# Another order of the steps of all five engines, and other PSUM banks, in a mixer and feed-forward kernel on one core

## The reference, cut to what matters

```python
# x: 4 batches of 512 rows of 512; W1, W3: 2048 x 512; W2: 512 x 2048
def mixer(h, Wi, Wf, Wg, Wo, gnorm_w):
    i, f, g = h @ Wi.T, h @ Wf.T, h @ Wg.T
    gate = sigmoid(f)
    v = silu(i) * (1 - gate)
    o = scan over the rows t of a batch: o[t] = gate[t] * o[t-1] + v[t]
    o = o * rsqrt(mean(o * o) + eps) * gnorm_w * g * sigmoid(g)
    return o @ Wo
def ffn(x, W1, W2, W3):
    hidden = silu(x @ W1.T) * (x @ W3.T)
    hidden = fwht(hidden)                  # Walsh-Hadamard over 2048, / sqrt(2048)
    return hidden @ W2.T
x = x + layernorm(mixer(layernorm(x)))
return x + layernorm(ffn(layernorm(x)))
```

## Time and profile before

| what | value |
|---|---|
| time, median of 3 runs | 689.96 us (690.3, 688.73, 689.96) |
| profiled execution, its time | 689.71 us |
| profiled execution, its span | 687.9 us |
| TensorE busy | 656.9 us (95%) |
| VectorE busy | 409.8 us (60%) |
| ScalarE busy | 352.8 us (51%) |
| GpSimd busy | 234.1 us (34%) |
| mean granted clock of TensorE | 0.995 |
| moved by DMA | 114.12 MB |

### The profile page before, as it was taken

How to read it: one execution, slowest core, us unless ns; L and a number is a source line. 1 busy time by engine, 2 the same in 40 slices (tenths; PEclk the granted TensorE clock), 3 DMA queues, 4 the chain that set the end, 5 groups by cost and what they waited for, 6 DMA issues and landing times.

```text
span 687.9 us, 11542 instructions
## 1 busy us (share of the span) xinstructions
PE 656.9 (95%) x4339; PEld 427.8 (62%) x4340; DVE 409.8 (60%) x791; ACT 352.8 (51%) x629; POOL 234.1 (34%) x216
## 2 busy tenths in 40 slices
...
GB/s 318 406 404 103 129 117 62 61 7 179 122 160 132 169 280 146 329 300 113 266 274 174 111 108 108 136 299 224 108 108 126 170 134 192 146 120 200 3 1 91
DMA packets 60743, 114.12 MB, mean 166 GB/s; under 512 B 40464, under 2 KB 40720, under 8 KB 56080
## 3 DMA queue, kind: packets, MB, share of 16 engines
...
...
## 4 chain that ended last, share of the span: by engine, by line
PE 64%; DVE 16%; ACT 7%; issue 5%; DVEq 3%; DMA 2%; POOL 2%; SPq 0%; POOLq 0%; ACTq 0%
PE ps L635 21%; PE ps L636 21%; PE ps L637 21%; DVEq L1052 3%; DVE st L1051 2%; ACT junk L914 1%; DVE o_s L1142 1%; ACT ring L835 1%; DMA out<-res 1%; DVE w2t L1306 1%; DVE w2t L1311 1%; DVE mv L1053 1%; ACT junk L921 1%; POOL w2t L1406 1%; DVE ring L1251 1%
## 5 line engine op out<-in xcount | busy, mean ns | idle before, releaser
L635 PE MATMUL ps<-xb,ring 128*128 128x256 f16 (+1 forms) x704 | 212.6, 302 | 3.5 <-DVE ring L1094 1.6
L637 PE MATMUL ps<-xb,ring 128*128 128x256 f16 (+1 forms) x704 | 212.6, 302 | 0.0
L636 PE MATMUL ps<-xb,ring 128*128 128x256 f16 (+1 forms) x704 | 212.6, 302 | 0.0
L1421 POOL TENSOR_TENSOR ring<-sga,ring 128x512 f16<-128x512 f32 x64 | 78.5, 1232 | 316.9 <-ACT ring L1007 316.9
L635 PE MATMUL ps<-ring 128*128 128x256 f16 x384 | 105.2, 274 | 4.4 <-DVE ring L1281 4.3
L636 PE MATMUL ps<-ring 128*128 128x256 f16 x384 | 105.0, 274 | 0.0
L637 PE MATMUL ps<-ring 128*128 128x256 f16 x384 | 105.0, 273 | 0.0
L635 PE MATMUL ps<-w2t,ring 128*128 128x512 f16 x256 | 97.0, 379 | 3.2 <-POOL ring L1421 3.2
L637 PE MATMUL ps<-w2t,ring 128*128 128x512 f16 x256 | 97.0, 379 | 0.0
L636 PE MATMUL ps<-w2t,ring 128*128 128x512 f16 x256 | 97.0, 379 | 0.0
L635 PEld LDWEIGHTS ps<-xb,ring 128*128 128x128 f16 x704 | 69.1, 98 | 40.8 <-issue 3.7
...
## 6 DMA issues: line engine op xcount, KB each, us to landing
...
```

Of the source, the lines that this page charges most:

```text
L635: pe.matmul(dst, a_hi, b_hi, start=start, stop=False, skip_group_check=onto)
L636: pe.matmul(dst, a_hi, b_lo, start=False, stop=False, skip_group_check=onto)
L637: return pe.matmul(dst, a_lo, b_hi, start=False, stop=stop, skip_group_check=onto)
L1421: pool.tensor_tensor(hid(b, c, 1), sga[:, c % 2], hid(b, c, 0), ALU.subtract).then_inc(hid_lo, 1)
```

## The change

Only the five tables differ (L38 to L179). They hold the same steps. Their order differs on every engine, and many products have another bank. A line or two of the tables, from the first feed-forward batch change and from the end:

```diff
 PE_ORDER = """
...
-GQ.1.4:4 D.1.7 GP.1.5:6 GU.1.3 GR.1.4 GU.1.4 GQ.1.5:5 D.1.8 D.1.9 D.1.10 D.1.11 D.1.12 D.1.13 GR.1.5 GP.1.6:7 D.1.14
+GQ.1.2:4 D.0.62 GR.1.2 GU.1.1 GP.1.3:7 D.0.63 GU.1.2 GQ.1.3:5 GP.1.4:6 GR.1.3 GQ.1.4:4 D.1.0 D.1.1 GP.1.5:7 GR.1.4
+D.1.2 D.1.3 GU.1.3 D.1.4 D.1.5 D.1.6 GU.1.4 GQ.1.5:5 D.1.7 GP.1.6:6 GR.1.5 D.1.8 D.1.9 GQ.1.6:4 GU.1.5 GR.1.6 D.1.10
...
+D.3.37 D.3.38 GQ.3.15:5 D.3.39 GR.3.15 D.3.40 D.3.41 D.3.42 GU.3.15 D.3.43 D.3.44 D.3.45 D.3.46 D.3.47 D.3.48 D.3.52
 DVE_ORDER = """
...
-W.0.1 GU.1.2 GR.1.3 GU.1.3 W.0.2 W.0.3 UP.1.2 Z1.3.0 Z1.3.1 Z2.3.0 Z2.3.1 Z1.3.2 UP.1.3 GR.1.4 Z1.3.3 GU.1.4 Z2.3.2
+W.0.1 V.0.3 W.0.2 GR.1.3 GU.1.3 UP.1.2 W.0.3 GR.1.4 GU.1.4 Z1.3.0 UP.1.3 Z2.3.0 Z1.3.1 Z1.3.2 Z2.3.1 Z2.3.2 ZT.3.0
```

More of the change, by code:

```diff
@@ L44 @@
[L44 to L48, removed]
@@ new lines @@
+F.0.2:5 I.0.0:6 I.0.1:0 I.0.2:1 F.0.3:7 XT.1.2:2 G.0.0:3 G.0.1:6 G.0.2:5 I.0.3:4 G.0.3:2 XT.1.3:3 H2.0.0:0 H2.0.1:7
+F.1.0:6 G.1.0:1 I.1.0:5 MS.0.0:3 Y.0.0:4 Y.0.1:2 Y.0.2:3 Y.0.3:6 F.1.1:4 WS.0.0:1 I.1.1:5 G.1.1:2 F.1.2:1 I.1.2:4
+G.1.2:3 F.1.3:6 I.1.3:5 F.2.0:2 W2S.0.0:1 G.1.3:4 I.2.0:3 G.2.0:6 F.2.1:5 H2.1.0:2 H2.1.1:1 H2.2.0:0 H2.2.1:4 MS.1.0:7
+Y.1.0:3 Y.1.1:6 Y.1.2:5 Y.1.3:2 I.2.1:1 G.2.1:0 F.2.2:4 I.2.2:7 H2.3.0:3 H2.3.1:6 G.2.2:5 F.2.3:2 I.2.3:1 F.3.0:0
+G.2.3:4 I.3.0:7 G.3.0:5 MS.2.0:3 Y.2.0:2 Y.2.1:6 H2.4.0:0 Y.2.2:1 H2.4.1:4 Y.2.3:7 F.3.1:5 I.3.1:3 G.3.1:2 F.3.2:0
@@ new lines @@
+H2.5.0:4 H2.5.1:6 I.3.2:5 G.3.2:1 F.3.3:7 I.3.3:0 GP.0.0:6 G.3.3:3 GP.0.1:7 H2.6.0:2 GQ.0.0:4 GQ.0.1:5 GR.0.0 GR.0.1
+H2.6.1:1 MS.3.0:0 Y.3.0:3 Y.3.1:2 GP.0.2:6 GU.0.0 GU.0.1 GP.0.3:7 H2.7.0:1 Y.3.2:0 GQ.0.2:4 H2.7.1:3 Y.3.3:2 GR.0.2
+GQ.0.3:5 GP.0.4:6 GR.0.3 GU.0.2 D.0.0 GU.0.3 GP.0.5:7 D.0.1 GQ.0.4:4 D.0.2 D.0.3 D.0.4 D.0.5 GR.0.4 D.0.6 GQ.0.5:5
+D.0.7 GR.0.5 GU.0.4 D.0.8 D.0.9 D.0.10 D.0.11 GP.0.6:6 GU.0.5 D.0.12 GP.0.7:7 D.0.13 GQ.0.6:4 D.0.14 D.0.15 GR.0.6
+GQ.0.7:5 D.0.16 GR.0.7 D.0.17 D.0.18 D.0.19 GU.0.6 GU.0.7 GP.0.8:6 GP.0.9:7 GQ.0.8:4 D.0.20 D.0.21 D.0.22 GR.0.8
@@ new lines @@
+D.1.33 GR.1.12 D.1.34 D.1.35 GU.1.12 GP.1.13:7 D.1.36 D.1.37 GQ.1.13:5 D.1.38 GR.1.13 D.1.39 D.1.40 GU.1.13 GP.1.14:6
+GP.1.15:7 GQ.1.14:4 GQ.1.15:5 GR.1.14 D.1.41 GR.1.15 D.1.42 D.1.43 D.1.44 GU.1.14 D.1.45 D.1.46 D.1.47 GU.1.15
+GP.2.0:6 D.1.48 D.1.49 D.1.50 GP.2.1:7 D.1.51 D.1.52 GQ.2.0:4 D.1.53 D.1.54 D.1.55 D.1.56 GR.2.0 GU.2.0 GP.2.2:6
+D.1.57 D.1.58 GQ.2.1:5 D.1.59 GR.2.1 GU.2.1 D.1.60 GP.2.3:7 D.1.61 D.1.62 D.1.63 GQ.2.2:4 GQ.2.3:5 GR.2.2 GR.2.3
+GU.2.2 GP.2.4:6 GU.2.3 GP.2.5:7 GQ.2.4:4 D.2.0 D.2.1 GQ.2.5:5 GR.2.4 D.2.2 GR.2.5 D.2.3 GU.2.4 GP.2.6:6 GU.2.5 D.2.4
@@ new lines @@
+GP.2.7:7 D.2.5 D.2.6 GQ.2.6:4 D.2.7 GQ.2.7:5 D.2.8 GR.2.6 D.2.9 GU.2.6 D.2.10 GR.2.7 D.2.11 D.2.12 GU.2.7 GP.2.8:6
+D.2.13 GP.2.9:7 D.2.14 GQ.2.8:4 D.2.15 D.2.16 D.2.17 GR.2.8 GQ.2.9:5 D.2.18 GR.2.9 GP.2.10:6 D.2.19 GU.2.8 D.2.20
+D.2.21 GU.2.9 GQ.2.10:4 D.2.22 D.2.23 GP.2.11:7 D.2.24 GR.2.10 D.2.25 GU.2.10 GP.2.12:6 D.2.26 GQ.2.11:5 D.2.27
+GR.2.11 D.2.28 GU.2.11 D.2.29 GP.2.13:7 D.2.30 GQ.2.12:4 D.2.31 GR.2.12 D.2.32 D.2.33 D.2.34 GP.2.14:6 D.2.35 GU.2.12
+GQ.2.13:5 D.2.36 D.2.37 D.2.38 GQ.2.14:4 D.2.39 GR.2.13 D.2.40 D.2.41 GU.2.13 GP.2.15:7 D.2.42 GR.2.14 D.2.43
@@ L88 @@
[L88 to L90 removed]
+XT.0.0 XT.0.1 AQ.0.0 XT.0.2 XT.0.3 AQ.1.0 AQ.2.0 AT.0.0 AT.0.1 AQ.3.0 AT.0.2 AT.0.3 F.0.0 AT.1.0 AT.1.1 F.0.1 AT.1.2
+XT.1.0 AT.1.3 AT.2.0 AT.2.1 WN.0.0 AT.2.2 WN.1.0 AT.2.3 I.0.0 AT.3.0 I.0.1 AT.3.1 XT.1.1 WN.2.0 F.0.2 S.0.0 I.0.2
```

199 lines of the change are left out of this document (90 added, 109 removed).

## The result

The changed kernel takes 685.15 us (median of 7 runs, 683.37 to 687.67) against 689.96 (7 runs, 688.73 to 691.63). The ratio is 0.9932, with a 95% interval of 0.9912 to 0.9952: some 4.7 us faster. That lies inside the range, 677.8 to 686.0, and 4.2 us above the forecast of 681.0. The profiled execution took 684.75, with a span of 683.0.

A forecast was written before the change was run, and what follows sets the result against it. TensorE, busy 656.9 of 687.9 us, bounds the kernel, so an order can win only the other 31.0. 687.9 - 5.8 - 3.4 - 0.5 + 1.0 = 679.2 us of span, with 1.8 around it 681.0 us; range 677.8 to 686.

The forecast's parts named there:

- The end: TensorE's wait on GpSimd before D.3.56, after GU.3.15: seven D steps kept for this place cover it, -3.4 us.
- The middle: TensorE's wait before GU.1.4: copies moved ahead of the statistics on VectorE win 4.4 plus 1.4 of lower clock, -5.8 us.
- rival B: Batch change: late reloads hold VectorE at W.0.3 or Z1.3.3, giving back 2 to 5.8 us; 683 to 687, chance 0.14.
- The forecast's own interval: Whole kernel: the forecast holds at 679.5 to 682.5 us, chance 0.60.
- the signs named: TensorE: no wait over 1 us after 82, clock 1.00 from 20 us, D.3.56 right behind D.3.52, waits near 15 us.
- The clock: TensorE's lower clock after the middle wait loses 1.4 us, booked as won; the end's 3.2 us wait cost no clock.
- The front: Up to 82 us: VectorE's chain sets TensorE, so 0 booked, with bounds of -0.8 and +0.8 us.
- Small waits: ScalarE's copies holding TensorE between 195 and 275 us: -0.5 us booked.
- the 1.0: Products closer together: 0.2 us each at GP.1.2, GP.2.2, GP.3.2, plus 0.4 at the last batch change, +1.0 us.
- rival E: VectorE, tight in 200 to 290 us: its stretching grows and is exposed, making the kernel slower, near 691.5; chance 0.04.

The follow-up runs named there:

- b_end: Kernel before with seven D steps kept back until after GU.3.15 on TensorE; 688.89 us against 691.23, ratio 0.9967.
- a_end_undone: Changed kernel with the seven D steps put back in front of GU.3.15 on TensorE; 688.66 us, ratio 0.9958 to the kernel before.
- b_copies_first: Kernel before with the copies GR.1.4 and GU.1.4 moved ahead of the statistics (Z1.3.0) on VectorE; 694.71 us against 691.23, ratio 1.0055.
- b_slot_late: Kernel before with the load of weight slot WL.1.3 moved from ahead of O.0.0 to behind LZ.3.2 on SyncE; 692.12 us, ratio 0.9996.
- a_up_first: Changed kernel with UP.1.3 moved ahead of Z1.3.0 on VectorE; 686.44 us, ratio 0.9938 to the kernel before.
- a_copies_back: Changed kernel with the copies GR.1.4 and GU.1.4 put back behind Z1.3.2 on VectorE; 689.51 us, ratio 0.9962 to the kernel before.

## Why the prediction was right in its range and wrong in one step

**The end: right.** -3.4 was booked, and the column "end" fell from 3.40 to 0.10. b_end and a_end_undone show it from both sides. What the prediction took for safe, that such a wait doesn't cost the clock, was wrong (below), so where the lower clock follows the wait, the step is worth 1.5 to 1.8 us more (4.90 with 3.40 of wait in b_copies_first, 5.08 with 3.39 in b_slot_late, 4.84 with 3.06 in a_end_undone).

**The middle: the step that failed.** The prediction said of the statistics that "what waits for them is the input of the third batch", and booked -5.8. It followed GR.1.4, GU.1.4 and then GR.1.5, but not UP.1.3, which the new table puts behind Z1.3.0 on VectorE. Through UP.1.3 the seed of GP.1.5, and so GQ.1.5, waits for the first reload; the excerpt of the changed order shows it (L1332 behind the first L1051). UP.1.3 once moved ahead, a second path comes up that the sum left out too: at GR.1.5 it counted VectorE's queue only, but GR.1.5 also needs the copy L970, which stands on ScalarE behind ZT.3.0 and ZT.3.1 (a_up_first: 2.74 us). The middle fell by 0.9 us in the first profile of the changed kernel and by 3.3 in the second. b_copies_first shows that moving the two copies, on which the sum rested, costs 3 us by itself; a_copies_back that it does pay in the new order, where TensorE comes to GR.1.4 5 us earlier, which is the likely reason. This was rival B ("the reloads bite in another place"), which had 0.14 and named 683 to 687. It held in kind, by a third place: neither W.0.3 (it did wait 4.2 us, covered) nor Z1.3.3.

**The range was met with the help of a rival.** The forecast's own interval, 679.5 to 682.5 with 0.60, did not come. 685.15 lies in the range because the range had been drawn over most of B, and 0.85 us under its upper end; one of the seven executions, 687.67, was outside. Of the saving that was booked, 9 us, 4.8 came, of which the end gave 3.3 and the middle, in the profiled execution, 0.9. Of the signs named, D.3.56 follows D.3.52 as said, but one wait of over 1 us stands behind 82 us, the clock is not at full level throughout, and TensorE's waits sum to some 20 us by the list, between the 25 of before and the 15 named.

**The clock: half right.** The 1.4 us behind the middle wait was read rightly from the earlier trace rows (by start distances some 1.5: 6.03 less 4.42 and a few tenths of short waits), but was booked as gone with the wait. A new wait of 3.07 us brought it back in one profile, one of 2.21 in another did not.

**The front: right, as far as its spread lets it be told.** 0 was booked. WS.0.0 starts between 81.5 and 83.1 in the profiles with the new tables (nine of them) and between 81.8 and 84.0 in those with the old (five).

**Small waits: right in sum.** Up to GP.1.0 the losses fell from 2.28 to 1.54, -0.7 against -0.5 booked, and in the stretch from GP.1.11 they rose by 0.3 against 0.8 booked (0.2 of the 1.0, GP.1.2, stands in the middle and cost nothing to speak of). GP.3.7 was late by 0.2 to 0.5, with 0.3 forecast. GP.2.2 and GP.3.2 cost too little to stand out.

**VectorE's stretch (rival E) grew in one place and did not come to the time.** The split of L1248 takes 1168 ns on average in the changed kernel where it took 997, but the larger split L1268 takes 1348 in place of 1499, and VectorE's busy time in that window is 86.7 us, as before; no wait on L1281 or over 0.6 us on L961 stands there. The stretch goes with GpSimd: in the changed kernel the six splits of L1248 that overlap an instruction of GpSimd take 1.31 to 1.64 us, and the five that overlap none 0.74. Before, three took 1.64 to 1.75, each beside such an instruction, and eight 0.73 to 0.75, seven of them beside none.

```profile
L1248 DVE SCALAR_TENSOR_TENSOR ring<-ring,w_s 128x512 f16<-128x512 f32 x11 | 12.6, 1168 | 0.0
```

The account of the two profiled executions, in their spans: front -0.3, small waits up to GP.1.0 -0.7, middle -0.9, behind it +0.3, end -3.3; together -4.9, which is the difference of 687.9 and 683.0. What the other PSUM banks do by themselves no run shows.
